# Gathering unpadded chunks: 784 gathers and 832 lots on a path instead of 832 padded chunks

## What is computed

```
h   = relu(layernorm(x))
xn  = batchnorm(h, norm1)
agg = segment_sum(xn[src], dst) / max(deg, 1)       # deg: edges that end at a node
conv = relu(agg @ W_conv + b_conv)
# attention with random features over one dense block of 256 nodes, then the output:
out = x + batchnorm(conv + h_attn + h, norm2)
```

## Time and profile before

| | us |
|---|---|
| median of three runs | 3114.46 |
| profiled execution | 3113.11 |
| its span | 3111.3 |
| TensorE busy | 2468.4 (79%) |
| VectorE busy | 2432.8 (78%) |
| ScalarE busy | 1040.9 (33%) |
| GpSimd busy | 1890.3 (61%) |
| granted TensorE clock, mean | 0.931 |

### The profile page before, as it was taken

How to read it: one execution, slowest core, us unless ns; L and a number is a source line. 1 busy time by engine, 2 the same in 40 slices (tenths; PEclk the granted TensorE clock), 3 DMA queues, 4 the chain that set the end, 5 groups by cost and what they waited for, 6 DMA issues and landing times. The chain is left out here.

```text
span 3111.3 us, 45478 instructions
## 1 busy us (share of the span) xinstructions
PE 2468.4 (79%) x11200; PEld 1539.0 (49%) x11201; DVE 2432.8 (78%) x4175; ACT 1040.9 (33%) x3233; POOL 1890.3 (61%) x1927
## 2 busy tenths in 40 slices
PE   1698736988989898989878899777777777779990
PEld 1355525766767676767656733333333333334440
DVE  9999998988989898988887567766666666666658
ACT  5644334555555555555546700000000000001220
POOL 0000007777777777777746467777777777775667
PEclk6799867999999999999998899999999999999995
DMA  5011027787878787877757867777777777774227
GB/s 195 32 44 44 36 72 231 235 240 234 244 235 243 229 244 236 243 235 231 243 192 257 289 184 211 210 210 210 210 210 210 210 210 210 210 211 139 64 57 283
DMA packets 227574, 601.74 MB, mean 193 GB/s; under 512 B 57441, under 2 KB 57441, under 8 KB 227481
## 3 DMA queue, kind: packets, MB, share of 16 engines
q0 software_dynamic: 136960, 456.11, 50.5%
q1 hardware_dynamic: 90520, 144.66, 13.8%
HBM read 546.53 MB, written 54.10 MB: 193 GB/s over the span
## 5 line engine op out<-in xcount | busy, mean ns | idle before, releaser
L499 POOL DMA_INDIRECT big<-feat_table,idx x880 | 840.0, 955 | 745.4 <-ACT idx L521 447.5
L1087 POOL DMA_INDIRECT big<-h_table,idx x728 | 688.5, 946 | 242.5 <-issue 211.4
L792 PE MATMUL psA<-big,onehot 128*128 128x260 f32 x1760 | 451.7, 401 | 16.0 <-DVE big L675 13.9
L792 PE MATMUL psB<-big,onehot 128*128 128x260 f32 x1760 | 434.8, 390 | 7.3
L547 ACT ACTIVATE big<-big,late_weights 128x65 f32<-128x65 f32 x1760 | 434.0, 340 | 0.0
L792 PEld LDWEIGHTS psA<-big,onehot 128*128 128x128 f32 x1760 | 325.4, 195 | 103.9 <-issue 37.0
L792 PEld LDWEIGHTS psB<-big,onehot 128*128 128x128 f32 x1760 | 318.2, 191 | 64.4 <-DVE acc L685 17.6
L521 ACT CAST idx<-minorB 128x8 int32 (+1 forms) x108 | 21.7, 203 | 910.0 <-DMA big<-h_table,idx 679.0
L1725 PE MATMUL psA<-big,onehot 128*128 128x512 f32 x488 | 241.8, 619 | 79.7 <-DMA big<-h_table,idx 50.5
L1485 DVE TENSOR_TENSOR acc<-acc,psA 128x512 f32 x278 | 190.8, 686 | 126.2 <-PE psA L1725 67.9
L1725 PE MATMUL psB<-big,onehot 128*128 128x512 f32 x488 | 236.9, 608 | 65.7 <-DMA big<-h_table,idx 44.1
(11 more groups left out here) (404 smaller groups left out, 3999.4 us busy)
## 6 DMA issues: line engine op xcount, KB each, us to landing
nodes_all<-slot_nodes SPq DMA_DIRECT2D x56, 512.0 KB, 5.7
big<-feat_table,idx POOLq DMA_INDIRECT x880, 3.8
feat_table<-big SPq DMA_DIRECT2D x49, 264.0 KB, 2.1
x_table<-acc SPq DMA_DIRECT2D x49, 256.0 KB, 4.1
big<-h_table SPq DMA_DIRECT2D x49, 256.0 KB, 2.6
big<-x_table SPq DMA_DIRECT2D x49, 256.0 KB, 4.2
acc<-in_x_dram SPq DMA_DIRECT2D x4, 3072.0 KB, 17.5
big<-in_x_dram SPq DMA_DIRECT2D x48, 256.0 KB, 4.3
```

Of the source, the lines that this page charges most:

```text
L499: g.indirect_dma_start(ring[:, b.k, q * SB + u, :], None, feat_table, bass.IndirectOffsetOnAxis(ap=idx[:, 2 * b.k + q, u:u + 1], axis=0)). ...
L792: ins = pet.matmul(psum[:, 512 * hf:512 * hf + HALF_W], onehot[:, q, u % SB, :], ring[:, b.k, u, HALF_W * hf:HALF_W * (hf + 1)], start=(u ...
L1087: g.indirect_dma_start(rows_l1[SB * r.place + b], None, h1_table, bass.IndirectOffsetOnAxis(ap=idx[:, r.place, b:b + 1], axis=0)).then_inc ...
```

## The change

B's pads per tile go: its edges are sorted without them, and only the end of the list is padded. So a chunk may hold edges of several tiles. 98 rows of 8 chunks, 784, are gathered. A lot is now one chunk for one tile; 784 chunks and 48 steps to a next tile make a path of 832 lots. Before each lot either the chunk or the tile advances by one.

The path is computed on the chip between the layers. VectorE compares the first tile of each chunk with the tile numbers (`crossed`); TensorE sums the comparison (`ranks`, how many chunks begin before a tile); VectorE compares lot numbers with the ranks (`beyond`, 48 x 832); TensorE sums that into each lot's tile; VectorE subtracts it from the lot number, which gives each lot's chunk (`own_chunk`). From this come tables in SBUF: the lot's tile, its place in the ring, per four lots how many groups of chunks must have arrived, and per group of chunks after how many lots it is free. The nodes of each lot's chunk, less 128 times its tile, are made with `chosen` masks by GpSimd and `select` matmuls by TensorE, and ScalarE copies them into `nodeB`. A node outside of the lot's tile equals none of 0 to 127, and adds nothing.

The ring has 24 chunks, all in `big`. GpSimd waits for `freed`, which SyncE counts up in a loop of its own with thresholds read from the table. TensorE reads the ring places of four lots and their arrival count into registers. ScalarE passes arrivals on in order (`arrived`), and VectorE keeps the counts. Several buffers move.

```diff
-LOT, LOT1 = 256, P
+LOT = 256
...
+CHUNK_ROWS = -(-E // COLS)
+CHUNKS_B = CHUNK_ROWS * SB
+ROWS1 = (CHUNKS_B + TILES - 1) // SB
+LOTS1 = ROWS1 * SB
...
-            act.wait_ge(fields, 3)
-            s.copy(tileB.rearrange("p r b -> p b r"),
-                   wk1.bitcast(I32)[0:1, :].rearrange("p (b r) -> p b r", r=P)).then_inc(sortB_done, 1)
-            act.wait_ge(fieldsT, 4)
-            s.copy(nodeB[:, :, :].rearrange("p b r -> p (b r)"), psB[:, :]).then_inc(sortB_done, 1)
+            act.wait_ge(fields, 2)
+            s.copy(sorted_nodes, wk1.bitcast(I32)).then_inc(sortB_done, 1)
...
+        RING1, CYCLE, CHUNK_CYCLE = 24, 12, 3
+        GROUPS1 = RING1 // 4
@@ SyncE, after the attention @@
+            with sp.Fori(0, RELEASES // 2) as i:
+                for u in range(2):
+                    sp.wait_ge(lot1_ps, load_count(sp, release, i, u, LOTS1 + LOT1_CREDIT))
+                    sp.sem_inc(freed, 1)
@@ GpSimd, before it clears acc @@
+            PD.wait(pool, "chunks")
+            SPE.wait(pool, "diag")
+            for b in range(SB):
+                if b >= 2:
+                    PP.wait(pool, f"select{b - 2}")
+                PG.done(g.tensor_scalar(chosen[b % 2], own_chunk, float(b), None, ALU.is_equal), f"chosen{b}")
@@ GpSimd, gather_row @@
-                    pool.wait_ge(lot1_ps, r(SB, 4 * hf + 4))
+                    if r.i is not None or r.c >= CHUNK_CYCLE:
+                        pool.wait_ge(freed, r(2, hf + 1 - GROUPS1))
@@ ScalarE: after projT; before keep_uk; before exp_q; in the loop @@
+            PA.done(s.copy(node_rows, sorted_nodes), "nodes")
...
+            PD.wait(act, "own")
+            s.copy(table_rows[0:1, 0:HALF1], psD[0:1, 0:HALF1])
+            PA.done(s.copy(table_rows[0:1, HALF1:LOTS1], psE[0:1, 0:HALF1]), "tiles")
...
+            PP.wait(act, f"select{SB - 1}")
+            for n, ps in enumerate((psD, psE)):
+                ins = s.copy(nodeB[:, :, n * ROWS1 // 2:(n + 1) * ROWS1 // 2].rearrange("p b r -> p r b"),
+                             ps[:, 0:HALF1].rearrange("p (r b) -> p r b", b=SB))
+            PA.done(ins, "slots")
...
+                for u in range(2):
+                    act.wait_ge(h_arrived[(2 * r.c + u) % GROUPS1], r.turn(64, 64))
+                    act.sem_inc(arrived, 1)
+                put_indices(minorB, r(1, CHUNK_CYCLE), r.c % CHUNK_CYCLE, idx3)
@@ VectorE: before x1; after slot 13; after ones_mat, in part @@
+            PD.done(v.tensor_tensor(crossed, first_tile.unsqueeze(2).broadcast_to([P, SB, TILES - 1]),
+                                    iota_row[:, 1:TILES].unsqueeze(1).broadcast_to([P, SB, TILES - 1]), ALU.is_lt), "first_tiles")
...
+            v.tensor_scalar(beyond, lot_numbers[0:TILES - 1, :], rank, None, ALU.is_ge)
...
+                ins = v.scalar_tensor_tensor(own_chunk[:, part], lot_numbers[:, part], first_of_row, ps[:, 0:HALF1],
+                                             ALU.subtract, ALU.subtract)
...
+            link(v.scalar_tensor_tensor(place_of_lot.rearrange("p r b -> p (r b)"), lot_numbers[32:33, :], float(D), second_part,
+                                        ALU.mult, ALU.add))
...
+            PD.done(v.tensor_scalar(quads, quad_group, 1.0, None, ALU.add), "chunks")
@@ VectorE, add_row @@
+                dve.wait_ge(counted1, r(1, 1))
+                v.tensor_copy(counts[:, bass.ds(r(SB, 0), SB)], counts_ps).then_inc(counts_kept, 1)
@@ TensorE, during the grams and in sum_row @@
+                if 13 <= t < 13 + SB // 2:
+                    select(2 * (t - 13))
+                    select(2 * (t - 13) + 1)
+            PA.wait(pe, "slots")
...
-                        pe.wait_ge(h_arrived[r.place][b // 4], r.turn(64, 64))
+                        at = load_places(pe, r(1, 0), b)
+                        pe.wait_ge(arrived, load_count(pe, needed_by_quad, r(1, 0), b // 4, 2 * CHUNK_ROWS))
-                    pet.matmul(lot1_sums(r, b), onehot[:, r.q, b, :], rows_l1[SB * r.place + b],
+                    pet.matmul(lot1_sums(r, b), onehot[:, r.q, b, :], big[:, bass.ds(at[b % 4], D)],
                                start=True, stop=True).then_inc(lot1_ps, 1)
@@ the start @@
-            destination_fields = split_tiles(sortB, raw_dst)
+            v.tensor_scalar(sortB.bufs[:, 1, :], sortB.bufs[:, 0, :], signs[:, 0:1], None, ALU.mult).then_inc(sortB.step, 1)
-            mark_tiles(*destination_fields, 2)
-            count_tiles(2)
-            pad_and_start(sortB, 2, LOT1)
```

## The result

The changed kernel takes 3088.18 us (median of 4 runs, 3086.09 to 3088.49) against 3112.52 us for the kernel before (4 runs): 0.9920 of its time, 95% interval 0.9903 to 0.9937, some 24.3 us less. Forecast were 3077 us, 37.6 us less than the 3114.46 us that stood then for the kernel before.

The account below looks back on a forecast made before the run. GpSimd's gather issue was taken to bound layer 1. Gains of 1.5 us (layer 0) and 49.6 (gathers), less 13 (stage before) and 0.5 (tail), gave 37.6 off 3113.11: 3075.5, as median 3077; range 3068 to 3084.

Parts of the forecast that it names:

- What bounds: Layer 1's gathers and sums: GpSimd's steady issue sets the pace, 1.2513 us a step.
- The start, nothing: Kernel start: some 10.4 us less VectorE work, all lost in its wait for ScalarE's statistics; gain 0.
- Layer 0, 1.5 us: Layer 0's start: ScalarE's shorter preparation and fewer late first lots gain 1.5 us, bounds 0 and 4.5.
- The stage before the gathers, 13 us: Between the layers: new table work loses 13 us, 11 on VectorE and 2 on ScalarE; bounds 2 and 26.
- I add 3 us: VectorE's 14 linked table operations: 3 us added to 7.9 for running beside GpSimd's scaling, making 11.
- taken 0: Eight small operations before x1, about 1.6 us, lie under VectorE's 1.48 us wait for GpSimd; cost 0.
- my bound of 2.1: Stage before the gathers: GpSimd makes each `chosen` mask in 0.7 to 2.1 us.
- They are not made up, since the DMA engines are full behind: Stage before the gathers: DMA engines are full from 1690 to 1730 us, so a late start is not recovered.
- the attention ... and the 28 gathers under it are otherwise untouched: Attention after 1766 us and the first 28 gathers under it: otherwise unchanged, no cost added.
- The gathers: Layer 1's loop: 832 gathers become 784 at an unchanged 1.25 us step; 50 us gained.
- The tail: Last gather issue to last sum: 7.2 us plus 0.5 for ScalarE's relay.
- selects on ScalarE's path: Rival, stage before the gathers: ScalarE waits for the `select` matmuls, 11 us more, 3088; chance 0.17 with other delays.

Follow-up runs that it names:

- e9: Changed kernel plus 18 memsets on VectorE ahead of its wait for ScalarE's statistics at the start; 3086.43 us, 0.9918 of the kernel before.
- e2: Changed kernel with ScalarE's slot copies behind two exponentials and the fifth group's square root; 3651.63 us on the stalling chip, 0.9978 of the kernel before.
- e6: Changed kernel with VectorE's one-row block behind the 34th x1 tile, scratch row in its own place; 3076.67 us, 0.9891 of the kernel before.
- e7: Changed kernel with the one-row block late and VectorE's leave for TensorE's first counts early; 3071.87 us, 0.9879 of the kernel before.
- e10: Changed kernel with TensorE loading each quad's four ring places twice, 208 more register loads; 3086.54 us, 0.9914 of the kernel before.
- e8: Changed kernel with 62 more gathers of 128 rows in layer 1's loop, into an unread place; 3162.19 us, 1.0167 of the kernel before.
- e3: Changed kernel with VectorE's leave for the first counts ahead of its subtractions; 3652.87 us on the stalling chip, 0.9975 of the kernel before.
- e4: Changed kernel with late block (scratch row overlapping x), later slot copies and early counts leave; 3639.59 us on the stalling chip, 0.9935 of the kernel before.
- e11: Changed kernel with 93 of 744 loop gathers left out, all 832 lots still summed; 2971.63 us, 0.9542 of the kernel before.
- e1: Changed kernel with the one-row block behind the 34th x1 tile, scratch row overlapping x; 3645.43 us on the stalling chip, 0.9954 of the kernel before.

## Why the prediction came out 11 us too low

- **What bounds: right.** GpSimd's issue paces layer 1. 62 more gathers cost 76.4 us, 93 fewer gain 117.
- **The start, nothing: right.** The wait took all of it (e9).
- **Layer 0, 1.5 us: not contradicted.** The last reciprocal of layer 0 came 1.8 us earlier in one trace against one; the spread of 5 us over nine traces (above) doesn't allow more.
- **The stage before the gathers, 13 us: right in kind, too small by 4.** The VectorE block took 12.9 us, not 11. The step "I add 3 us" for work beside GpSimd was mis-sized: alone the block's eleven operations are 6.7 us, beside GpSimd 11.4, so the contention is 4.7. "SBUF — State Buffer" of the Trainium skill, section "SBUF: two separate sides", describes the port pair that the two engines lock against each other. The runs agree in kind (0.58 against 1.32 us an operation, and GpSimd's median 1.39 against 1.05), and the loss of 0.74 us an operation is less than the whole GpSimd operation of 1.04 us by which I had worked out 19 us. The larger part, at nothing in the sum, is TensorE's diagonals, 2.5 us longer at a granted clock of 0.50; no run took them out. And of the 1.8 us gained in layer 0 only 0.6 is left when TensorE starts its last matmuls ahead of the diagonals (1658.30, 1658.94 before): "taken 0" for the small operations there is not borne out, and what took the 1.2 us is open. ScalarE's two slot copies took 3.8 us instead of 1.1, and GpSimd's selections 2.3 to 2.8 us, above my bound of 2.1. ScalarE did wait for the last selection, 1.54 us of the 11 that the rival named. The copies' order gained nothing in e2, on the stalling chip; on a quiet chip it was not tested alone. "They are not made up, since the DMA engines are full behind": right for this stage, and e6 shows the other side of it. Once the block lay in an idle time, 9.1 us came back.
- **The loop's entry: not in the sum.** Taken over unchanged from before were the counts' start, the first loads and the first matmuls. They cost 1.9, 1.4 and, with a granted clock of 0.54, 2.3 us over the forecast; the attention ahead of them took another 1.5, of which the cause is open (TensorE's mean granted clock over its last 25 us was 0.73, 0.82 before). With 3.8 from the stage ahead (4.1 less 0.3 in layer 0) that makes the 10.9. e7 got back 4.8 by moving one semaphore increment. The step that failed is "the attention ... and the 28 gathers under it are otherwise untouched": I had followed VectorE's leave for the counts and the register loads only where the loop is running, not at its first turn.
- **The gathers: right to 1 us**, 948.7 us against 949.7. Register loads are hidden (e10), the ring never holds GpSimd after gather 24, and VectorE's row is shorter than forecast, 8.04 us.
- **The tail:** +3.3 us where 0.5 was taken. 2.1 lie ahead of VectorE's last sum, and a part differs from run to run: most of the other traces have 298 us, which would be +2.

The sum: 37.6 forecast, less 10.9 at gather 24, plus 1.0 in the loop, less 2.8 in the tail: 24.9, as the profiles have it. The rival "selects on ScalarE's path" named 3088, the right time for the wrong reason: the late stage was mostly the block and the clock, and ScalarE waited 1.54 us for the selects, not 11. The gain came out at two thirds of the forecast because several small costs outside the loop all went one way, while the bound inside it was read rightly.

## What to carry to other kernels

Small one-row table work belongs into a measured idle time of its engine where GpSimd is quiet, and not ahead of the pass that feeds the DMA engines: the same eleven operations cost 11.4 us in one place, and moved to the other they gave 9.1 us back. Where a ring restarts a bound engine, follow every wait of the first turn one by one, for each is paid in full there, and with the clock of the engine that waited. A saving in the bound resource was forecast to 2% (e8: 1.23 of 1.25 us a gather); what it took to prepare the saving was not: the stage ahead cost 17.1 us against 13, and the loop's entry 5.6 that stood in no sum.

## What I had not expected of the hardware

- One-row VectorE operations of 832 columns: 0.58 us alone, 1.32 beside GpSimd's elementwise work; with two inputs 1.01 and 1.75. GpSimd's own went from a median of 1.05 to 1.39 us.
- GpSimd's comparison of 128x832 floats with a constant takes 2.28 us with little beside it and up to 2.80.
- 3.2 us in which TensorE did almost nothing (1.78 + 1.38, between short bursts) were followed by 3.6 us at 0.54 of the full clock; with the gaps cut to 0.71 us the granted clock stayed at 1.00. Ahead of the diagonals 3.31 us without work were followed by 7.0 us at 0.50 in nine traces of kernels with the change, but in four others (e2, e3, e4, e11) the first sixteen matmuls behind the same gap ran at full clock and all 32 took 5.2 to 5.4 us: such a gap doesn't cost the clock each time, and what decides it is open.
- One chip ran the kernel before 18% slower, at mean granted clocks of 0.85, with stalls of up to 9 us put down to "issue". There GpSimd waited for free places in the loop, 154 us in e1's trace up to 3000 us beside the wait ahead of gather 24, and its issue was no longer the bound all the time. What stalls it is open.
